# A four-layer decoder on one core: the latent attention's output projection moved into its loop, and two changes of order

## The reference, cut to what matters

```python
x = layernorm(x + attn(x))                 # 0: 16 heads, rotary, causal
x = layernorm(x + routed_by_token(x))      # 1: SwiGLU, one of four experts
x = layernorm(x + mixture_of_low_rank(x))  # 2
x = layernorm(x + state_space_scan(x))     # 3
x = layernorm(x + latent_attention(x))     # 4: the change
x = layernorm(x + moe_top6_of_16(x))       # 5

# latent attention (4): 16 heads of 128, q latent 96, kv latent 64
scores = (q_nope @ k_nope + q_rope @ k_rope) * scale     # window of 8 keys by token id
out = concat_heads(softmax(scores) @ v) @ W_o
```

## Time and profile before

| | |
|---|---|
| median of 3 runs | 720.73 us (720.21 to 721.47) |
| the profiled execution's own time | 719.47 us |
| its span in the profile | 717.1 us |
| PE busy | 666.0 us, 93% of the span |
| DVE busy | 464.6 us, 65% |
| ACT busy | 349.2 us, 49% |
| POOL busy | 345.6 us, 48% |
| mean granted clock of PE | 0.981 |
| chain that ended last | PE 78%, DVE 14%, ACT 4% |

### The profile page before, as it was taken

One profiled execution on the slowest core, in us unless ns is written; L12 is line 12 of the kernel. 1 busy time (PEld: TensorE's weight loads), 2 busy tenths in 40 slices (PEclk: granted clock), 3 DMA queues, 4 the chain that ended last, 5 costly groups with the idle time before them and its releaser, 6 DMA issues.

```text
span 717.1 us, 12719 instructions
## 1 busy us (share of the span) xinstructions
PE 666.0 (93%) x4596; PEld 518.1 (72%) x4596; DVE 464.6 (65%) x1081; ACT 349.2 (49%) x807; POOL 345.6 (48%) x471
## 2 busy tenths in 40 slices
PE   5989889999999888888899999999999999999994
PEld 5856567856456555466778888878769888888884
DVE  4579868463144699997678877762546566556655
ACT  4655526241512765355689998880252322222234
POOL 5326416340101779445678888762344444445521
PEclk9999999999998999899899999999999999999998
DMA  8000007001003000000000000003011111111001
GB/s 277 1 2 3 1 1 294 1 1 48 0 1 83 1 16 1 0 1 1 1 1 2 3 0 3 1 2 111 0 45 45 45 46 60 49 45 45 1 1 59
DMA packets 10350, 23.30 MB, mean 32 GB/s; under 512 B 2033, under 2 KB 5074, under 8 KB 9906
## 3 DMA queue, kind: packets, MB, share of 16 engines
q1 hardware_dynamic: 10002, 22.24, 9.4%
q10 hardware_dynamic: 288, 0.26, 0.1%
HBM read 21.45 MB, written 1.05 MB: 31 GB/s over the span
## 4 chain that ended last, share of the span: by engine, by line
PE 78%; DVE 14%; ACT 4%; issue 2%; POOL 1%; DMA 1%; POOLq 0%; SPq 0%; DVEq 0%; ACTq 0%
PE psum L441 41%; DVE A L1447 6%; PE psum L1045 4%; PE psum L479 4%; PE psum L1058 4%; PE psum L502 4%; PE psum L821 2%; PE psum L459 2%; PE psum L866 2%; PE psum L553 2%; PE psum L595 1%; PE psum L569 1%; PE psum L694 1%; DVE stats L1194 1%; DVE A L1314 1%
## 5 line engine op out<-in xcount | busy, mean ns | idle before, releaser
L441 PE MATMUL psum<-parts 128*128 128x256 f32 (+2 forms) x1440 | 246.8, 330 | 8.9 <-DVE parts L1268 7.3
L441 PEld LDWEIGHTS psum<-parts 128*128 128x128 f32 (+1 forms) x1440 | 216.1, 192 | 36.8 <-DVE parts L1268 7.3
L2054 POOL TENSOR_SCALAR probs<-probs,row_rec 128x256 f32<-128x256 f32 x128 | 71.0, 568 | 32.7 <-DVE row_rec L1258 30.0
L1968 ACT ACTIVATE A<-psum 128x512 f32<-128x512 f32 x44 | 26.3, 598 | 115.6 <-PE psum L441 115.5
L1447 DVE TENSOR_TENSOR_SCAN A<-decay,psum 128x256 f32<-128x256 f32 x128 | 75.4, 661 | 5.9 <-PE psum L866 5.9
L1553 DVE TENSOR_TENSOR A<-A,psum 128x512 f32<-128x512 f32 x44 | 30.1, 686 | 71.3 <-ACT A L1968 58.4
L1656 ACT ACTIVATE probs<-probs,neg_max 128x256 f32<-128x256 f32 x128 | 63.7, 500 | 19.5 <-DVE neg_max L1249 19.5
L1249 DVE CUSTOM_DVE_ANT_0 probs<-psum,ctxT 128x256 f32<-128x256 f32 x128 | 48.9, 419 | 24.9 <-PE psum L441 23.1
L441 PE MATMUL psum<-parts,A_rounded 128*128 128x256 f32 x372 | 55.2, 284 | 1.5 <-DVE A_rounded L1388 1.5
L2209 POOL CAST parts<-C 128x512 fp32r<-128x512 f32 x22 | 13.4, 611 | 85.1 <-PE psum L441 74.9
L441 PEld LDWEIGHTS psum<-parts,A_rounded 128*128 128x128 f32 x372 | 49.1, 192 | 2.8 <-DVE A_rounded L1388 1.9
(11 more groups left out here) (246 smaller groups left out, 1286.6 us busy)
## 6 DMA issues: line engine op xcount, KB each, us to landing
C<-in_experts SPq DMA_DIRECT2D x22, 384.0 KB, 3.1
A<-in_w_o SPq DMA_DIRECT2D x1, 2048.0 KB, 11.7
x_tok<-in_x_tok SPq DMA_DIRECT2D x1, 1024.0 KB, 7.3
ctxT<-in_ctxT SPq DMA_DIRECT2D x1, 1024.0 KB, 10.9
A<-in_w_uqT SPq DMA_DIRECT2D x1, 768.0 KB, 5.7
out<-x_tok SPq DMA_DIRECT2D x6, 128.0 KB, 1.8
xT<-in_xT SPq DMA_DIRECT2D x2, 256.0 KB, 4.1
C<-in_wqk SPq DMA_DIRECT2D x1, 512.0 KB, 4.4
```

Source lines behind the costliest of these rows:

```text
L441: ins = mm(o, left[l], right[r], start=first and n == 0, stop=last and n == 2, skip_group_check=True)
L2054: last = pool.tensor_scalar(pr, pr, row_rec[:, u % RING[n], j:j + 1], 1.0, ALU.mult, ALU.mult)
```

## The change

1. **The projection goes into the loop.** `om` and the eight-tile `out4` are gone. ACT copies the result of `apply4` (now always in bank 4) as the high part into `om_parts`; DVE makes the low part from the same bank (`low_of_heads`, one new instruction a pair, at the start of each odd step); PE then multiplies by `vo_parts` in three rounded products for each of two token tiles (new `out4(g)`, six products a pair), adding into bank 6 over eight pairs. POOL makes `vo_parts` from `vo_fold` in steps 5, 7, ..., 19 (`split_outputs`). In each odd step PE waits for the low part of the pair before (`om_low`), then makes the products of `output_pairs(G)`, then applies pair G. The last three pairs' products stand behind the loop, the last one behind the first gate product.
2. **Most of layer 4's norm goes into the loop.** DVE makes the residuals of two tiles at u = 28, 44 and 60 and normalises the first half at u = 49 and 51; POOL's `rstd_of` stands at u = 46; PE turns the first half at u = 61; ACT copies it out and rounds it at u = 62, 63 and 65. The experts' loads start when the first sequence's tiles are out, into other places of A and C.
3. **Order in the head of the loop.** POOL's `rstd_of(3, (1,))` moves from behind `add_pair` at u = 4 to the start of u = 3; PE's turn moves from u = 6 to u = 7; `sums_out(1)` on ACT moves from ahead of the loop to behind the first exponentials, and ACT's copy of `apply4`'s result from behind the exponentials to ahead of them.
4. **Order at the end of layer 0.** `back_to_tokens` and `token_heads` of tiles 2 to 5 move ahead of the last heads; tiles 6 and 7 stand at `out0` 2 and 3. Layer 1's first two `up` make both high parts first, and `low_of_x` stands behind residual 6 instead of 7.

The semaphore `q_split` is renamed `w_split` throughout; those lines are left out.

```diff
@@ -194,7 +194,8 @@
...
 key_parts = [view(C_rounded, 3584, [P, 2, T]), view(parts, 8192, [P, 2, T])]
-om = view(A, 0, [P, NPAIR, T])
+om_parts = view(A_rounded, 0, [P, NPAIR, 2, S])
+vo_parts = view(A_rounded, 4096, [P, 2, NPAIR, D])
@@ -229,9 +230,9 @@
...
 hid1 = view(A, 10240, [P, AHEAD, HALF])
-gateT = view(A, 14336, [NE, T])
-cwT = view(A, 15360, [PAD, T])
-raw = [view(C, (GU + DN) * r, [P, GU + DN]) for r in range(RAW)]
+gateT = view(A, 0, [NE, T])
+cwT = view(A, 1024, [PAD, T])
+raw = [view(t, at, [P, GU + DN]) for t, at in ((A, 14336), (A, 15104), (C, 2688), (C, 0))]
@@ -319,7 +320,7 @@
...
 QUERIES_AT = {2 * (n - FIRST) + 4: n for n in range(FIRST, B * NPAIR)}
-TURNS_AT, LATENTS_AT = {6: 2, 9: 3}, 11
+TURNS_AT, LATENTS_AT = {7: 2, 9: 3}, 11
@@ -331,7 +332,14 @@
...
-    return bank[{1: (4, 5, 5, 7), 3: (4, 5, 6, 4)}.get(k, (4, 5, 4, 5))[q]]
+    return bank[{1: (4, 5, 5, 7), 3: (4, 5, 6, 6), 4: (5, 7, 4, 6)}.get(k, (4, 5, 4, 5))[q]]
+LN4_AT = 61
+def output_pairs(G):
+    place = (G - 3) % NPAIR
+    return () if G < 3 or place == 0 else (G - 4, G - 3) if place == 1 else (G - 3,)
@@ -422,6 +430,8 @@
...
     for c in range(FCH):
+        if c == RAW - 1:
+            sp.wait_ge(sem("a4_av"), B * NPAIR)
@@ -504,11 +514,13 @@
...
             if G is not None:
+                if G >= 1:
+                    pe.wait_ge(sem("om_low"), G)
+                for g in output_pairs(G):
+                    out4(g)
...
                 pe.wait_ge(sem(n + "pTd"), AT_ONCE[n] * (G + 1))
-                if G >= 2:
-                    pe.wait_ge(sem(n + "oT"), G - 1)
-                apply(G, bank[(4, 6)[G % 2]]).then_inc(sem(n + "av"), 1)
+                apply(G, bank[4]).then_inc(sem(n + "av"), 1)
@@ -654,6 +666,8 @@
...
             to_features(0)
+            back_to_tokens(2)
+            back_to_tokens(3)
@@ -661,6 +675,9 @@
...
             turn_with_maxima(o + 1).then_inc(sem("a0_qm"), 1)
+    to_features(1)
+    back_to_tokens(4)
+    back_to_tokens(5)
@@ -668,9 +685,9 @@
...
     def out0(i, o):
-        if i + 2 < NT:
-            back_to_tokens(i + 2)
-        if i + 1 < NT:
+        if i in (2, 3):
+            back_to_tokens(i + 4)
+        if 2 <= i + 1 < NT:
@@ -707,7 +734,11 @@
...
     pe.wait_ge(sem("r_ctx"), 4)
-    for k in range(11):
+    up_high(0)
+    up_high(1)
+    up_low(0)
+    up_low(1)
+    for k in range(2, 11):
@@ -1004,17 +1035,18 @@
...
             if u == 9:
-                pe.wait_ge(sem("a4_oT"), 1)
+                pe.wait_ge(sem("ln_xT"), 4 * 3 + 3)
             ln_transposes(3, 1, (TURNS_AT[u],))
-        if u == 9:
-            pe.wait_ge(sem("ln_xT"), 4 * 3 + 3)
         if u == LATENTS_AT:
-            pe.wait_ge(sem("a4_oT"), 2)
...
             query_pair(n)
+        if u == LN4_AT:
+            pe.wait_ge(sem("q_mul"), B * NPAIR)
+            pe.wait_ge(sem("q_lat"), B * NPAIR)
+            ln_transposes(4, 0)
@@ -1047,19 +1079,26 @@
...
+    def out4(g):
+        b, p = g // NPAIR, g % NPAIR
+        if b == 0:
+            pe.wait_ge(sem("w_split"), 3 + p + 1)
+        elif p == 0:
+            pe.wait_ge(sem("ln_r"), 8 * 4 + 2 * b)
+        for j in range(2):
+            last = product3(bank[6][:, j * D:(j + 1) * D],
+                            [om_parts[:, p, r, j * P:(j + 1) * P] for r in range(2)],
+                            [vo_parts[:, r, p, :] for r in range(2)], p == 0 and j == 0, p == NPAIR - 1)
+            if p == NPAIR - 1:
+                last.then_inc(sem("fin"), 1)
...
     attention("a4_", scores4, apply4, False, (0, 1), next_queries)
-    pe.wait_ge(sem("a4_oT"), B * NPAIR)
-    def out4(i, o):
-        for p in range(NPAIR):
-            last = mm(o, om[:, p, i * P:(i + 1) * P], vo_fold[:, p, :], start=(p == 0),
-                      stop=(p == NPAIR - 1))
-        return last
-    close(4, out4)
+    out4(B * NPAIR - 3)
+    out4(B * NPAIR - 2)
@@ -1142,6 +1177,8 @@
...
     gate_rows(0)
+    pe.wait_ge(sem("om_low"), B * NPAIR)
+    out4(B * NPAIR - 1)
@@ -1213,8 +1250,8 @@
...
             residual(k, i, scale, place)
-        if between:
-            between()
+            if between and i == 6:
+                between()
@@ -1234,7 +1271,10 @@
...
         U = 2 * B * NPAIR
-        for u in range(U + LAG[n] + 2):
+        for u in range(U + LAG[n] + 4):
+            g = group_at(n, u - LAG[n] - 3 - 2 * AT_ONCE[n])
+            if g is not None:
+                low_of_heads(g)
@@ -1353,10 +1393,12 @@
...
-    token_heads(0)
-    token_heads(1)
+    for i in range(4):
+        token_heads(i)
...
     heads_out(OCTS - 2)
+    token_heads(4)
+    token_heads(5)
@@ -1372,7 +1414,7 @@
...
-    norm(0, 1.0, fin_bank, lambda i: token_heads(i + 2) if i + 2 < NT else None, low_of_first_half)
+    norm(0, 1.0, fin_bank, lambda i: token_heads(i + 4) if i in (2, 3) else None, low_of_first_half)
@@ -1517,6 +1559,14 @@
...
+    def low_of_heads(g):
+        dve.wait_ge(sem("a4_oT"), g + 1)
+        tt(om_parts[:, g % NPAIR, 1, :], bank[4][:, 0:S], om_parts[:, g % NPAIR, 0, :].bitcast(f32), ALU.subtract
+           ).then_inc(sem("om_low"), 1)
+    out4_bank = lambda i: bank[6][:, (i % 2) * D:(i % 2 + 1) * D]
@@ -1535,12 +1585,21 @@
...
             query_low(1)
+        if u in (28, 44, 60):
+            for i in ((u - 28) // 8, (u - 28) // 8 + 1):
+                residual(4, i, 1.0, out4_bank)
+        if u in (49, 51):
+            for i in (u - 49, u - 48):
+                normalise(4, i)
...
     attention("a4_", False, (0, 1), rotate_next)
-    norm(4, 1.0, fin_bank)
+    for i in (6, 7):
+        residual(4, i, 1.0, out4_bank)
+    for i in range(4, NT):
+        normalise(4, i)
@@ -1913,13 +1972,12 @@
...
             j = n - 28
-            act.wait_ge(sem("q_split"), 3)
+            act.wait_ge(sem("w_split"), 3)
...
     latent_pair(3)
-    sums_out(1)
@@ -1932,6 +1990,8 @@
...
     def latent_next(u):
+        if u == 0:
+            sums_out(1)
@@ -1942,23 +2002,26 @@
...
             query_high(1)
+        if u in (LN4_AT + 1, LN4_AT + 2):
+            ln_out(4, 0, (u - LN4_AT - 1,))
+        if u == LN4_AT + 4:
+            operands(0)
...
     def out_of4(g):
-        b, p = g // 8, g % 8
-        return om[:, p, b * S:(b + 1) * S], bank[(4, 6)[g % 2]][:, 0:S]
-    attention("a4_", False, (0, 1), out_of4, latent_next)
+        return om_parts[:, g % NPAIR, 0, :], bank[4][:, 0:S]
...
-        ln_out(4, half)
...
+    attention("a4_", False, (0, 1), out_of4, latent_next)
...
         act.wait_ge(sem("m_lgT"), half + 1)
-        af(gateT[:, half * HALF:(half + 1) * HALF], bank[6][0:NE, :], ACT.Copy).then_inc(sem("m_rows"), 1)
+        af(gateT[:, half * HALF:(half + 1) * HALF], bank[5][0:NE, :], ACT.Copy).then_inc(sem("m_rows"), 1)
@@ -1974,9 +2037,9 @@
...
-    operands(0)
...
     silu(0)
+    ln_out(4, 1)
@@ -2188,14 +2251,27 @@
...
     def add_next(u):
+        if u == 3:
+            rstd_of(3, (1,))
...
             key_low(u - 12)
+        if u in range(5, 5 + 2 * NPAIR, 2):
+            split_outputs((u - 5) // 2)
+        if u == 46:
+            rstd_of(4, (0,))
...
             add_pair(QUERIES_AT[u])
-        if u == 4:
-            rstd_of(3, (1,))
+    def split_outputs(p):
+        if p == 0:
+            pool.wait_ge(sem("fold_out"), 6)
+            pool.wait_ge(sem("s_z"), 8)
+        link(pool.tensor_copy(vo_parts[:, 0, p, :], vo_fold[:, p, :]))
+        pool.tensor_tensor(vo_parts[:, 1, p, :], vo_fold[:, p, :], vo_parts[:, 0, p, :].bitcast(f32), ALU.subtract
+                           ).then_inc(sem("w_split"), 1)
@@ -2204,6 +2280,8 @@
...
         pool.wait_ge(sem(f"ld_raw{c % RAW}"), 16 * (c // RAW + 1))
+        if c == 0:
+            pool.wait_ge(sem("q_l"), B * NPAIR)
@@ -2217,8 +2295,8 @@
...
     for half in range(2):
-        rstd_of(4, (half,))
         if half:
+            rstd_of(4, (half,))
...
         pool.wait_ge(sem("operand_hi"), X_AT + half + 1)
```

More of the change, by code:

```diff
@@ L695, in up, with up_low @@
                            start=(r == 0 and c == 0), stop=False)
+            def up_low(k):
+                half, e, fc = k // 8, k // 2 % 4, k % 2
+                o, hh = bank[k % 4][:, :], slice(half * HALF, (half + 1) * HALF)
                 pe.wait_ge(sem("r_xlo"), 2 * (half + 1))
@@ L1095, in gate_rows @@
                     pe.wait_ge(sem("m_rows"), 1)
[L1096 to L1097 removed]
                 for c in range(DC):
[L1099 removed]
+                    last = mm(bank[5][0:NE, :], wgateT[:, c, :], xT[:, c, half * HALF:(half + 1) * HALF],
                               start=(c == 0), stop=(c == DC - 1))
@@ L1646, in attention @@
                         copy_probs(act, n, v, causal_keys, lambda o, i: af(o, i, ACT.Copy), "a")
+                    G = group_at(n, u - LAG[n] - 2 - 2 * AT_ONCE[n])
+                    if G is not None:
+                        act.wait_ge(sem(n + "av"), G + 1)
+                        dst, src = out_of(G)
+                        af(dst, src, ACT.Copy).then_inc(sem(n + "oT"), 1)
```

(7 more changed lines are left out.)

18 lines of the change are left out of this document (8 added, 10 removed).

## The result

| | before | after |
|---|---|---|
| median, same chip | 720.89 us (4 runs) | 732.71 us (727.91 to 736.51, 4 runs) |
| the same kernel again (e12) | 719.23 us (7 runs) | 730.85 us (727.98 to 733.00, 4 runs) |
| profiled execution, its span | 719.47, 717.1 us | 734.72, 732.7 us |
| mean granted clock of PE | 0.981 | 0.971 |

The changed kernel is slower by 1.7%: ratio 1.0171, 95% interval 1.0131 to 1.0211; the second time 1.0155 (1.0101 to 1.0209). The forecast was 722.5, with 712.5 to 730 as the range. The sign was right, the size too small by 10 us.

The account below looks back on a forecast made before the run. The prediction took PE to bound the kernel, saturated in the loop. Gains of 31.7 us against costs of 33.5 gave +1.8 on the 719.47 us profiled execution; moving the 720.73 median equally gave 722.5 us, range 712.5 to 730.

Parts of the forecast that it names:

- part 1: Output products: three rounded products replace each full-precision one, adding 0.74 us of PE time a pair in the loop.
- part 2: Behind the loop: 35.8 us of PE's path become 11.5, so 24.3 us leave; PE idle about 2.6.
- part 4: PE's wait in the loop for DVE's low part: 0.05 us a plain pair, 1.3 us for 27 pairs, plus extra places.
- Bursts: DVE's residuals ahead of the low part stall PE at u = 29, 45 and behind u = 60: 6.0 us.
- Masks: Window masks alone on DVE at u = 26 and 42 delay the low part: 0.6 us.
- The drain: Behind step 64, where ACT rounds the first half between two copies: 0.6 us.
- part 5: POOL splitting the projection's weights in steps 5 to 19 delays its additions: 2.5 us, bounds 0 to 5.
- rival B: New pauses take PE's clock down, two of them costing 3.0 us each: 728.5 us, chance 0.16.
- parts 6 and 7: New orders: the loop's head gains 5.9 us by losing its pause and half clock; layer 0's end gains 1.5.
- Rival C: The head's pause only moves to u = 8 to 12, halving that gain: 725.5 us, chance 0.14.
- Rival A: DVE's low part is in time, so most waiting costs in the loop fall away: 713.0 us, chance 0.27.

Follow-up runs that it names:

- e12: The changed kernel once more, unedited, for a second profile and a second median: 730.85 us, ratio 1.0155.
- e8: Changed kernel with spread residuals, later query-latent low part and moved wait, plus second expert's weight split and products put into the last pause: 708.02 us.
- e6: Changed kernel with PE's wait on `om_low` moved behind the output products, directly ahead of the application: 721.89 us.
- e4: Changed kernel with layer 4's residuals one at a time and the query latents' low part a step later: 720.69 us.
- e9: Changed kernel with the moved wait, and POOL's weight splits at u = 11 to 25 in place of 5 to 19: 723.53 us.
- e2: Kernel before the change with the new order in the head of the loop alone: 714.06 us, ratio 0.9917.
- e1: Kernel before the change with the new order at the end of layer 0 alone: 718.97 us, ratio 0.9983.
- e11: The 708.02 us kernel (e8) without the change of order at the end of layer 0: 709.47 us, ratio 0.9847.
- e7: Changed kernel with both the spread residuals and later query-latent low part (e4) and the moved wait (e6): 713.86 us.
- e5: Kernel before the change with both changes of order, loop head and layer 0, and no projection in the loop: 713.53 us.

## Why the prediction was right in sign and too small in size

**Product (part 1), right.** 0.74 us a pair was forecast; without waits a pair costs 5.30 - 4.585 = 0.72.

**Behind the loop (part 2), right but for the clock.** 35.8 us became 12.0 (forecast 11.5), with PE idle for 2.89 + 0.55 (forecast 2.6). The clock of 0.77 behind it (535 to 540 us) cost another 1.3, and e8 shows the price of the whole: 5.8 us.

**Plain pairs (part 4), mis-sized.** The wait for the low part was put at 0.05 us a pair, with 0.15 as the upper end; it was 0.13. The earlier trace rows gave the right reading, that DVE's low part and PE meet within 0.1 us, but I compared it with the application at 452.58, and the products now stand ahead of it, 0.4 us behind the turn. The 0.08 us too little make 1.8 us over some 22 pairs.

**Bursts (part 4), right.** 2.3 at u = 29 and 45 and 1.4 at u = 61 were forecast; 1.97, 1.97 and 1.44 were measured. Masks: 0.6 forecast, 2 x 0.28 measured. The drain was put at 0.6 and cost 1.5, the wait again, as e6 shows.

**POOL's splits and u = 13 (part 5), mis-sized.** Against the plain 5.43, and against e4's 6.32 and 4.80 for the pairs with two and with no products, G = 2 to 6 cost 1.9 + 1.2 + 0.1 + 0.1 + 0.45 = 3.8 us, where 2.5 were forecast. The bound of 5 held. The mechanism was only a part: the splits made 1.3 of the pause's 1.97 us (e9). Behind the rest stands the row of DVE's 2.3 us. The prediction listed who waits for `om_low`, but not each wait that DVE already had ahead of the new instruction.

**Clock (rival B), the step that failed.** I gave 0.16 to the case that the new pauses take the clock down. Both profiles of the changed kernel show it behind all three pauses of 2 us and behind the last one. Each fall cost 1.2 us, not the 3.0 that I took from the earlier trace rows: 1.24, 1.25 and 1.19 at G = 3, 11 and 19, and 1.3 behind the loop. One of them is in the 3.8 of part 5, so 2 x 1.2 in the loop and 1.3 behind it were missing. So the step that failed is the zero at which the sum put the clock behind the new pauses; the wait in plain pairs (0.05 for 0.13) and the drain (0.6 for 1.5) are the two terms that were mis-sized with it. Rival B's 728.5 is nearer, but by 2 x 3.0 in place of four falls of 1.2 to 1.3: its mechanism was right and its price wrong.

**Head and layer 0 (parts 6 and 7), right.** 5.9 forecast, 5.9 measured in e2; 1.5 forecast, 0.95 in e1. Rival C, that the head's pause only moves, is refuted by the changed kernel itself: ahead of the pause at u = 13 its list of waits has nothing above 0.4 us between 342 and 364 us. e2, which has no splits, could not test it.

Added up, the loop cost 39.6 us where the parts came to 33.5: plain pairs 1.8, drain 0.9, part 5 1.3, clock 2.4, less 0.6 for the bursts, 5.8 together; 0.3 stay open, and the sizes are rough. From the forecast's +1.8 to the +15.6 between the two spans are 13.8 us, and the stretches above give them: 6.1 in the loop, 0.5 and 1.4 behind it (the clock), 1.0 in the head, and 4.8 ahead of it, where +3.3 was measured and part 7 had -1.5. The 1.0 is the clock too: the head takes 20.9 to 21.0 us in the five profiles of this order in which the clock falls at its start (0.66 from 325 to 330 us here), and 19.6 in the seven in which it does not, 1.3 us less. So some 8 of the 13.8 us are the clock: 2.4 in the loop, 1.3 behind it, 1.3 in the head, and 3.4 ahead of it by the windows below.

**The 4.8 us ahead of layer 4 are in no edit.** The profiled execution was a late one, and much of this is chance. The first scores of layer 4 start at 326.5 us in it. In the nine other profiles that have the same order up to that point, they start between 321.3 and 326.9, on average of all ten at 323.6; in the four with layer 0 as before, between 322.8 and 325.0, on average at 323.8. Layer 2's code is the same in all. Windows there, before and then after:

```profile
190.00:195.00 5.00, 4.38 (x13) 1.00 0.00 0
195.00:200.00 5.00, 5.00 (x11) 1.00 0.00 0
...
190.00:195.00 5.00, 4.38 (x8) 0.76 0.00 0
195.00:200.00 5.00, 5.00 (x7) 0.56 0.00 0
```

PE is busy as long in both, at another granted clock. Its sum over the windows from 130 to 320 us, (1 - clock) x 5 us each, is 6.8 before and 10.2 in this profile of after, 8.5 in the second; in the other eleven kernels' profiles it goes from 5.1 to 12.0, though none of them touches this stretch. Those with layer 0's order average 8.0 in ten profiles, those without it 6.0 in four. Whether the shift of 1.3 us brings a part of this about, or only chance, I can't say: e11 was to show it and its interval is too wide. The two averages of the starts differ by 0.1 us only.

**What the loss is made of.** From the changed kernel, spreading DVE's work gives 9 to 10 us by the ratios (e4), the wait one place later another 6 (e7), and filling the last pause 5.8 (e8). The idea itself was sound: with these three, the kernel is at 708.0 us, 5.5 below the two changes of order without it (e5). How much of the 5.5 is the idea's own is less sure. In the two profiles, 5.9 us apart, 2.5 lie in the loop and behind it; the other 3.4 lie ahead of the first application, where PE has the same instructions in both, and where the clock fell more often in e5's. The fastest executions of the two kernels, 710.3 and 707.8, are 2.5 us apart as well. Rival A's 713 was the time of a kernel whose low part is in time; e7, where it nearly is, takes 713.9. That it comes so near is in part luck, since A's sum has no fall of the clock behind the loop, and e7's profile has one.

## What to carry to other kernels

When an instruction that PE waits for is put on another engine's list, read every wait that this engine already has ahead of the new place, also those that cost nothing so far, and spread work that comes in bursts. Put a wait directly ahead of the instruction that needs it: six independent products stood behind this one, and moving it was worth 6 to 9 us. This saturated loop gained nothing from the work moved in (+23.5 us in it and -23.5 behind it in e7), so what decided was the pauses that the move opened there and the one that it left behind.
